# Windowed-attention feed-forward block: a new order of each engine's step, and the query norms moved into the exponentials

## The reference

```python
def _layer(x, wqkv, qs, ksc, wo, lg, lb, w1, b1, w2, b2):
    h = shift_token(x)
    q, k, v = split(h @ wqkv)              # 8 heads of 64
    q = l2norm(q) * qs
    k = l2norm(k) * ksc
    q, k = rotary_xpos(q, k)
    o = local_attention(q, k, v)           # window 64, looks one window back, softmax(8 q k)
    x = x + o @ wo
    h = shift_token(x)
    h = (h - mean) / sqrt(var + 1e-05) * lg + lb
    a, g = split(h @ w1 + b1)              # 341 each
    return x + (a * gelu(g)) @ w2 + b2
```

## Time and profile before

| | |
|---|---|
| runs of the kernel | 5374.78, 5377.23, 5378.79 us |
| profiled execution: time, span | 5375.44 us, 5373.8 us |
| PE busy over the span | 4059.5 us (76%) |
| VectorE busy | 2944.3 us (55%) |
| ScalarE busy | 2609.7 us (49%) |
| GpSimd busy | 1836.0 us (34%) |
| feed-forward, first call, 1336 to 2296 us: PE, DVE, ACT, GpSimd busy | 706.02, 601.29, 518.27, 686.82 of 960 us |
| granted TensorE clock, mean | 0.856 of full speed |

### The profile page before, as it was taken

How to read it: one execution, slowest core, us unless ns; L and a number is a source line. 1 busy time by engine, 2 the same in 40 slices (tenths; PEclk the granted TensorE clock), 3 DMA queues, 4 the chain that set the end, 5 groups by cost and what they waited for, 6 DMA issues and landing times.

```text
span 5373.8 us, 103098 instructions
## 1 busy us (share of the span) xinstructions
PE 4059.5 (76%) x31924; PEld 2448.2 (46%) x31924; DVE 2944.3 (55%) x5889; ACT 2609.7 (49%) x6422; POOL 1836.0 (34%) x2053
## 2 busy tenths in 40 slices
PE   2999999995677777744666665999999547777776
PEld 1444444442445454422222222777777424545554
DVE  2555555554566666642444443666666646666664
ACT  1555555552455555513333333666666325555553
POOL 0000000001777777714222221111111157777774
PEclk9999999997899999965555555999999768999998
DMA  3222222221000000005999999777777210000001
GB/s 116 81 72 75 79 72 75 78 75 50 20 21 20 20 21 20 21 24 193 380 383 379 383 381 362 256 251 259 264 263 254 82 43 21 20 20 21 20 20 26
DMA packets 373727, 701.06 MB, mean 130 GB/s; under 512 B 53220, under 2 KB 160056, under 8 KB 373608
## 3 DMA queue, kind: packets, MB, share of 16 engines
q1 hardware_dynamic: 329576, 565.25, 30.8%
q0 software_dynamic: 44032, 134.30, 6.8%
HBM read 336.53 MB, written 314.64 MB: 121 GB/s over the span
## 4 chain that ended last, share of the span: by engine, by line
PE 40%; POOL 17%; issue 16%; DMA 12%; DVE 10%; POOLq 1%; ACT 1%; SPq 1%; DVEq 1%; ACTq 0%
DMA rel_k<-b_stage_k 11%; POOL f_rn L728 7%; PE ps L332 5%; PE ps L1461 5%; PE ps L1470 4%; PE ps L340 4%; PE ps L351 4%; PE ps L1452 3%; POOL f_rot L756 3%; PE ps L1481 2%; POOL f_p L766 2%; PE ps L1353 1%; DVE b_stage_k L1377 1%; DVE f_ss L1036 1%; PE ps L377 1%
## 5 line engine op out<-in xcount | busy, mean ns | idle before, releaser
L1377 DVE COPY b_stage_k<-ps 128x640 f32<-128x640 f32 (+2 forms) x512 | 359.0, 722 | 470.1 <-DMA rel_k<-b_stage_k 411.1
L430 ACT ACTIVATE a_p<-a_s,a_min 128x512 f32<-128x512 f32 x512 | 365.8, 715 | 471.4 <-DVE a_min L474 471.4
L1374 ACT ACTIVATE b_stage_q<-ps 128x640 f32<-128x640 f32 (+2 forms) x512 | 316.0, 624 | 505.9 <-PE ps L1356 389.0
L474 DVE CUSTOM_DVE_ANT_0 a_s<-ps,a_table 128x512 f32<-128x512 f32 x512 | 333.3, 688 | 409.6 <-PE ps L332 405.4
L1535 ACT ACTIVATE c_p<-c_s,c_min 128x512 f32<-128x512 f32 x512 | 370.2, 723 | 289.9 <-PE ps L1470 178.4
L1353 PE MATMUL ps<-b_e,b_st_k 48*128 48x512 bf16 (+1 forms) x512 | 305.9, 597 | 261.8 <-DVE b_stage_k L1377 261.8
L188 POOL COPY y<-ln_rows 128x512 f32 x32 | 19.9, 622 | 1361.5 <-DVE ln_rows L180 1361.5
L1570 DVE CUSTOM_DVE_ANT_0 c_s<-ps,c_rq 128x512 f32<-128x512 f32 x512 | 352.9, 689 | 202.5 <-PE ps L1461 187.6
L756 POOL TENSOR_TENSOR f_rot<-f_rc,f_rs 128x1024 f32<-128x1024 f32 x128 | 302.4, 2362 | 436.9 <-DVE f_rs L1027 436.6
L817 PE MATMUL ps<-ident,f_p 128*128 128x128 f32 x1024 | 171.0, 321 | 317.5 <-POOL f_p L766 314.3
L952 ACT ACTIVATE f_p<-f_s,f_min 128x128 f32<-128x128 f32 x1024 | 396.1, 393 | 0.3
(11 more groups left out here) (178 smaller groups left out, 9780.4 us busy)
## 6 DMA issues: line engine op xcount, KB each, us to landing
rel_q<-b_stage_q SPq DMA_DIRECT2D x64, 1280.0 KB, 7.8
rel_k<-b_stage_k SPq DMA_DIRECT2D x64, 1280.0 KB, 7.7
c_rq<-rel_q SPq DMA_DIRECT2D x64, 1024.0 KB, 7.4
c_rk<-rel_k POOLq DMA_DIRECT2D x64, 1024.0 KB, 11.8
a_table<-skew_bias SPq DMA_DIRECT2D x64, 896.0 KB, 4.6
f_vb<-f_v SPq DMA_DIRECT2D x256, 128.0 KB, 2.3
rel_k<-b_stage_k SPq DMA_DIRECT2D x32, 1024.0 KB, 9.4
rel_q<-b_stage_q SPq DMA_DIRECT2D x32, 1024.0 KB, 5.3
```

The costliest lines, as they stand in the source:

```text
L430: nc.scalar.activation(a_p[:, lt % 2, h, :], a_s[:, lt % 2, h, :], ACT.Exp, bias=a_min[:, lt % 2, h:h + 1], scale=-1.0, accum_out=a_sum[:, ...
L1377: moves_b1(dve, 1, lambda out, src: nc.vector.tensor_copy(out, src))
```

## The change

**Attention A:** `out_project` moves from quarter 2 to quarter 1, `add_to_x` from quarter 3 to quarter 2.

**Feed-forward, arithmetic:** queries are no longer multiplied by their inverse norm. Only the keys are (`f_kn`, half the size of `f_qk`); the unnormalised queries are transposed from `f_rot`, now with two buffers. The query's inverse norm, negated in `f_nq`, is the `scale` of the exponentials, and the minimum times the inverse norm (`f_bias`, a new VectorE operation) is their bias. The mask is scaled down once to fit. The Newton steps after both powers are dropped. The lower bound on the sums of squares becomes a `tensor_tensor` against a constant tile `f_eps` in place of a `tensor_scalar`.

**Feed-forward, order:** GpSimd scales the probabilities at the start of the next step (tile c) in place of at the end of this one (tile s2), and takes the layer norm's power there at m = 0. VectorE does `turn_heads` before it moves the probabilities, and normalisation, statistics and the inverted sums before the addition to x. TensorE projects v right behind q and k, transposes q and k before it mixes values, and computes the scores before `join_heads`, with two of the three MLP chunks, or `turn_x`, ahead of the scores. ScalarE moves the probabilities behind the first four exponentials, and the mixed values behind q and k.

```diff
@@ tensor_attn_a, vector_attn_a
-                if lt == 2 and done >= 2:
+                if lt == 1 and done >= 2:
                     out_project(s - 2, True)
...
-                if lt == 3 and done >= 2:
+                if lt == 2 and done >= 2:
                     add_to_x(s - 2)
@@ pool_ffn, step
-            if s2 is not None:
-                pool.wait_ge(f_inverted, upto(s2.g))
...
+            if c is not None:
+                pool.wait_ge(f_inverted, upto(c.g))
+                tt(f_p[:, c.par, :, :], f_p[:, c.par, :, :],
+                   f_rsum[:, c.par, :].unsqueeze(2).broadcast_to([P, HF, P]), ALU.mult).then_inc(f_p_ready, 1)
             if m == 0 and mlp is not None:
+                pool.wait_ge(f_lv_ready, upto_b(mlp.g))
+                pool.wait_ge(f_hn_ready, upto_b(mlp.g - 1, LT))
+                tt(f_rstd[:, :], f_lv[:, :], f_power[:, 0:LT], ALU.pow).then_inc(f_rstd_ready, 1)
...
+            if a is not None:
+                pool.wait_ge(f_turned, upto(a.g, 3))
+                pool.wait_ge(f_normed, upto(a.g - 2))
+                pool.wait_ge(f_qT_full, upto(a.g - 2))
+                tt(f_rot[:, a.par, :], f_rc[:, :], f_rs[:, :], ALU.add).then_inc(f_rotated, 1)
+                pool.wait_ge(f_ss_ready, upto(a.g))
...
+                tt(f_rn[:, m, :], f_ss[:, 1, :], f_power[:, :], ALU.pow).then_inc(f_rn_ready, 1)
...
+                tt(f_kn[:, :].rearrange("p (h d) -> p h d", d=DF),
+                   f_rot[:, a.par, INNER:2 * INNER].rearrange("p (h d) -> p h d", d=DF),
+                   f_rn[:, m, HF:2 * HF].unsqueeze(2).broadcast_to([P, HF, DF]), ALU.mult).then_inc(f_normed, 1)
+                hold(pool, f_exped, upto(a.g - 4, HF))
+                tt(f_nq[:, m, :], f_rn[:, m, 0:HF], f_minus[:, :], ALU.mult).then_inc(f_nq_ready, 1)
@@ scalar_ffn, exps
-                nc.scalar.activation(f_p[:, s2.par, n, :], f_s[:, s2.par, n, :], ACT.Exp, bias=f_min[:, s2.par, n:n + 1],
-                                     scale=-1.0, accum_out=f_sum[:, s2.par, n:n + 1]).then_inc(f_exped, 1)
...
+                nc.scalar.activation(f_p[:, s2.par, n, :], f_s[:, s2.par, n, :], ACT.Exp, bias=f_bias[:, s2.par, n:n + 1],
+                                     scale=f_nq[:, s2.m, head:head + 1], accum_out=f_sum[:, s2.par, n:n + 1]).then_inc(f_exped, 1)
@@ vector_ffn, mask_and_min, sum_squares
+            dve.wait_ge(f_rn_ready, upto(s2.g))
+            dve.wait_ge(f_minned, upto(s2.g))
+            tt(f_bias[:, s2.par, :].rearrange("p (h i) -> p h i", h=2), f_min[:, s2.par, :].rearrange("p (h i) -> p h i", h=2),
+               f_rn[:, s2.m, 0:HF].rearrange("p (i h) -> p h i", h=2), ALU.mult).then_inc(f_maxed, 1)
...
-            ts(f_ss[:, 1, :], f_ss[:, 0, :], L2_EPS, None, ALU.max).then_inc(f_ss_ready, 1)
+            tt(f_ss[:, 1, :], f_ss[:, 0, :], f_eps[:, :], ALU.max).then_inc(f_ss_ready, 1)
```

More of the change, by code:

```diff
@@ L849, in transpose_qk @@
                 for i in range(PAIRS_F):
-                    last = turn(ps[:, QK + k, i * P:(i + 1) * P], f_qk[:, k * INNER + i * P:k * INNER + (i + 1) * P],
-                                ident[:, :])
+                    src = f_kn[:, i * P:(i + 1) * P] if k else f_rot[:, b.par, i * P:(i + 1) * P]
+                    last = turn(ps[:, QK + k, i * P:(i + 1) * P], src, ident[:, :])
                 last.then_inc(full, 1)
@@ L871, in turn_normed, with mlp_up @@
             last.then_inc(f_hnT_full, 1)
-        def mlp_up(mlp, half, full):
-            for n, (at, w) in enumerate(CHUNKS):
+        def mlp_up(mlp, half, full, chunks):
+            for n in chunks:
+                at, w = CHUNKS[n]
                 mm(ps[0:w, PROBS + n, :], f_w1[:, mlp.layer, half * HID + at:half * HID + at + w], f_hnT[:, :],
@@ L903, in step @@
                 project_qk(a, b, s2, h)
+                project_v(a, h)
             if c is not None:
                 transpose_probs(m, c, mlp)
-            if a is not None:
-                project_v(a, h)
+            if b is not None:
+                transpose_qk(a, b)
             if c is not None:
                 mix_values(m, c, mlp)
+            if m == 1 and mlp is not None:
+                pe.wait_ge(f_hid_ready, upto_b(mlp.g - 1, 3))
+                pe.wait_ge(f_hnT_moved, upto_b(mlp.g))
+                mlp_up(mlp, 1, f_gate_full, (0, 1))
+            if m == 2 and mlp is not None:
+                pe.wait_ge(f_gelued, upto_b(mlp.g, 3))
+                mlp_up(mlp, 0, f_value_full, (0, 1))
+            if m == 3 and nxt is not None:
+                turn_x(nxt)
             if b is not None:
-                transpose_qk(a, b)
+                scores(b)
             if c is not None:
@@ L916, in step @@
             if m == 1 and mlp is not None:
-                pe.wait_ge(f_hid_ready, upto_b(mlp.g - 1, 3))
-                pe.wait_ge(f_hnT_moved, upto_b(mlp.g))
-                mlp_up(mlp, 1, f_gate_full)
+                mlp_up(mlp, 1, f_gate_full, (2,))
             if m == 2 and mlp is not None:
-                pe.wait_ge(f_gelued, upto_b(mlp.g, 3))
-                mlp_up(mlp, 0, f_value_full)
+                mlp_up(mlp, 0, f_value_full, (2,))
             if m == 3 and mlp is not None:
                 mlp_down(mlp)
-            if m == 3 and nxt is not None:
-                turn_x(nxt)
-            if b is not None:
-                scores(b)
         pe.wait_ge(f_zeros, F_ZEROS * (call + 1))
@@ L950, in exps @@
                 act.wait_ge(f_pT_full[1], upto(s2.g - 2))
-            for n in range(PAIRS_F * h, PAIRS_F * h + PAIRS_F):
-                nc.scalar.activation(f_p[:, s2.par, n, :], f_s[:, s2.par, n, :], ACT.Exp, bias=f_min[:, s2.par, n:n + 1],
-                                     scale=-1.0, accum_out=f_sum[:, s2.par, n:n + 1]).then_inc(f_exped, 1)
+            for i in range(PAIRS_F):
+                n, head = PAIRS_F * h + i, 2 * i + h
+                nc.scalar.activation(f_p[:, s2.par, n, :], f_s[:, s2.par, n, :], ACT.Exp, bias=f_bias[:, s2.par, n:n + 1],
+                                     scale=f_nq[:, s2.m, head:head + 1], accum_out=f_sum[:, s2.par, n:n + 1]).then_inc(f_exped, 1)
         def step(m, a, b, s2, c, ln, mlp, nxt):
@@ L960, in step @@
                                      ACT.Square).then_inc(f_squared, 1)
-            if c is not None:
-                act.wait_ge(f_pv, upto(c.g - 1))
-                act.wait_ge(f_pT_full[1], upto(c.g))
-                copy(f_pT[:, PAIRS_F:HF, :].rearrange("p i l -> p (i l)"), ps[:, PROBS + 1, :], f_pT_moved[1])
             if a is not None:
@@ L982, in step @@
                      ps[:, QK + 1, :].rearrange("p (i l) -> p i l", l=P), f_kT_moved)
+            if c is not None:
+                act.wait_ge(f_out_full, upto(c.g - 1))
+                act.wait_ge(f_pv, upto(c.g))
+                copy(f_oT[:, :], ps[:, MIXED, :], f_oT_moved)
             if s2 is not None:
@@ L1059, in step @@
                 mask_and_min(s2)
+            if a is not None:
+                turn_heads(a)
             if c is not None:
@@ L1064, in step @@
                                       ps[:, PROBS, :]).then_inc(f_pT_moved[0], 1)
+            if a is not None:
+                sum_squares(a)
             if m == 0 and mlp is not None:
                 normalize(mlp)
-            if a is not None:
-                turn_heads(a)
-                sum_squares(a)
-            if c is not None:
-                dve.wait_ge(f_out_full, upto(c.g))
-                tt(y[:, c.t, :], y[:, c.t, :], ps[:, V_BANK, 0:DIM], ALU.add).then_inc(f_x_mid, 1)
+            if m == 3 and ln is not None:
+                statistics(ln)
             if s2 is not None:
@@ L1076, in step @@
                 nc.vector.reciprocal(f_rsum[:, s2.par, :], f_sum[:, s2.par, :]).then_inc(f_inverted, 1)
+            if c is not None:
+                dve.wait_ge(f_out_full, upto(c.g))
+                tt(y[:, c.t, :], y[:, c.t, :], ps[:, V_BANK, 0:DIM], ALU.add).then_inc(f_x_mid, 1)
             if m == 2 and mlp is not None:
@@ L1083, in step @@
                         ALU.add, ALU.mult).then_inc(f_hid_ready, 1)
-            if m == 3 and ln is not None:
-                statistics(ln)
             if m == 3 and mlp is not None:
@@ L1094, in vector_ffn @@
         dve.wait_ge(f_const_loaded, 16 * F_CONST * (call + 1))
-        dve.wait_ge(f_tabled, (call + 1) * (4 * DEPTH))
+        dve.wait_ge(f_tabled, (call + 1) * (4 * DEPTH + 1))
         ffn_loop(dve, call, step)
```

81 lines of the change are left out of this document (32 added, 49 removed).

## The result

The changed kernel takes 5136.0 us (5126.5 to 5139.4, four runs), the kernel before beside it 5376.0 (5371.0 to 5378.8). The ratio is 0.9552, 95% interval 0.9535 to 0.9568. The forecast was 5135 us, range 5020 to 5230. That it came out to 1 us is luck: three terms of the sum were well off (m = 0, the clock, the steps in which a call fills) and their errors cancel.

A forecast was written before the change was run, and what follows sets the result against it. The feed-forward was taken as bound by a ring of GpSimd, TensorE and VectorE, 14.89 us a step, falling to 13.38. 5375.4 - 52 (attention A) - 190 (126 x 1.51) = 5133, plus 1.8: 5135 us, range 5020 to 5230.

The forecast's parts named there:

- Attention A, 52.0 us: Attention A: TensorE's waits for the addition to x at a unit's first projection all go, 52.0 us.
- GpSimd leaves the pace: Feed-forward: GpSimd's work falls to 8.7 us a step, its sum no longer waits for its scaled probabilities; something else sets pace.
- The new ring: Feed-forward: TensorE's pieces, squares and turn of heads follow each other, 9.70 us; with three MLP chunks at m = 1, 12.37.
- m = 0, 13.0 us: Feed-forward step m = 0: GpSimd's power blocks VectorE's normalising operations at the shared port, 13.0 us; without blocking 10.3.
- the first rival: Feed-forward m = 0: normalising operations run beside the power, 10.3 us; 5049 us total; chance 0.25, shared with a tighter ring.
- m = 2 and m = 3: Feed-forward: VectorE's work behind the output projection (m = 2) or the MLP's last product (m = 3) sets 14.2 and 13.3 us.
- The clock, 0.65 us a batch: Feed-forward: slow 1.2 GHz stretches of TensorE, expected fewer as idle gaps shorten, cost 0 to 1.3 us a batch, 0.65 taken.
- The steps in which a call fills: Feed-forward: three steps that fill and empty a call counted as unchanged; 1.51 us saved in each of 126 intervals.
- attention A without gain: Rival, attention A: the next wait in TensorE's queue is just behind, so nothing is gained; 5187 us, chance 0.04.
- the uncut ring: Rival, feed-forward: another handover closes the old ring; only Newton steps and half a product go, 2.33 us a step; 5031 us.
- The dearer port: Rival, feed-forward: the bias waits every step for the scaling of probabilities, up to 1.90 us; 5251 us; chance 0.2, shared.
- The slow clock: Rival, feed-forward: TensorE at 1.2 GHz; slower than before once 23% of its work falls into slow stretches; chance 0.03.

The follow-up runs named there:

- the run with two products earlier: Changed kernel with the first two products of the MLP's values ahead of the addition to x in VectorE's queue at m = 2: 5070.56 us, ratio 0.9432.
- that product moved: Changed kernel with the MLP's last product moved from m = 3 to the next m = 0, its addition to y behind the turn: 5061.81 us, ratio 0.9416.
- filling the gaps: Changed kernel with eight more identity transposes a step on TensorE, behind the transposes of the probabilities: 5068.42 us, ratio 0.9436.

## Why the prediction was right, and where it was not

- **Attention A, 52.0 us:** 54.9 alone, 55.2 in the changed kernel; no other wait took its place.
- **GpSimd leaves the pace, its sum 8.7 us:** right. It is 2.37 + 2.91 + 1.04 + 0.20 + 1.90 = 8.4 with 0.3 of handovers, and it idles 4.0 us before each rotary sum (256.1 us in 64). The half product took 1.04, not 0.95.
- **The new ring, m = 1 at 12.37 us:** 12.36 in the median of either call. The chain of TensorE's pieces, squares and turn is what the forecast said.
- **m = 0, 13.0 us: wrong.** The step that failed is that a power blocks the normalising operations: beside it they keep their median of 0.336 us, and the long instance that had spoken for it lay beside the addition of b2. The place of the port cost was the bias (0.97 us), which in the forecast "starts at or behind" the scaling; with m = 0 shorter than 13.0 it starts ahead of the scaling's end, so the first error hid the second. Measured 11.2 at full clock, 11.6 on average, in place of 13.0. That is the mechanism of the first rival (a free port), with a third of its gain paid back.
- **m = 2 and m = 3, 14.2 and 13.3 us:** right in mechanism (VectorE's queue behind the output projection, shown by the 0.65 us of the run with two products earlier, and behind the last product, shown by m = 3 with that product moved). At full clock 14.45 to 14.7 and 13.45 to 13.95, so the forecast was 0.3 to 0.5 and 0.2 to 0.6 short.
- **The clock, 0.65 us a batch: undersized.** The four intervals sum to 55.0 in the changed kernel and to 11.2 + 12.4 + 14.7 + 13.9 = 52.2 at full clock, so the clock takes 2.8 us; filling the gaps gave 2.0 of them back (53.0). I expected fewer slow stretches because TensorE's gaps became shorter; the gaps ahead of the transposes (3.24 us at 1684.98) are still there, and what follows them is in the ring now. The mechanism was on the list, at a quarter of its price.
- **The steps in which a call fills, 1.51 us each: undersized.** The first eight intervals of a call took 110.0 and 110.9 us, now 88.1 and 87.3: 2.8 a step, since nearly all of them lack the MLP, and a step is 11.0 us on average. That is 21 us more than counted.
- **The sum:** a full batch went from 60.2 to 55.0 us, 5.2 in place of 6.0, so the full batches give 23 us less than forecast; the filling steps give 21 more: 188 for 190. The nearness is luck, not a sign that the terms were right.

Of the rivals, attention A without gain is out by its run alone, and the uncut ring by the 217 us of the order alone. The dearer port is there, in full batches, at m = 0. The slow clock: means of 0.90 and 0.94 in the calls are 20 and 12% of the time at 0.50, so about 11 and 6% of TensorE's work, where 23% would have made the kernel slower. The rival "the order cuts nothing" put 2.33 us a step on the arithmetic alone; alone it gave 189.0 / 126 = 1.50, since m = 2 did not move (14.4 to 14.7); that another chain was level there already is the likely reason, which no run tests.

The Trainium skill (SBUF — State Buffer, Who interferes with whom) has a VectorE instruction with two SBUF inputs contend with a GpSimd instruction that reads SBUF, and the second of them blocked for the whole instruction. The bias behind the scaling (1594.44 and 1594.41) and line 1043 behind the sum agree. The power does not, in the changed kernel (GpSimd, then VectorE):

```profile
1367.85 1.01 POOL L748 TENSOR_TENSOR f_rstd<-f_lv,f_power 128x4 f32<-128x4 f32 x1
```

```profile
1368.56 0.17 DVE L1021 TENSOR_TENSOR f_bias<-f_min,f_rn 128x8 f32<-128x8 f32 x1
```

The bias, with two inputs in SBUF, took its usual 0.17 us inside the power.
